# Linear attention on one core: split float32r projections, a longer look-ahead, and rewritten engine lists with the inter-state products in one piece

## The reference, cut to what matters

```python
        def chunk_gla(q, k, v, gk, C=CHUNK):
            g = jnp.cumsum(gc, axis=1)
            g_last = g[:, -1]
            qg = qc * jnp.exp(g)
            kg = kc * jnp.exp(-g)
            A = jnp.einsum('cthd,cshd->chts', qg, kg)
            A = A * jnp.tril(jnp.ones((C, C), q.dtype))
            o_intra = jnp.einsum('chts,cshe->cthe', A, vc)
            k_out = kc * jnp.exp(g_last[:, None] - g)
            chunk_kv = jnp.einsum('cthd,cthe->chde', k_out, vc)
            decay = jnp.exp(g_last)

            def step(S, inp):
                kv, dec, qg_c = inp
                o_inter = jnp.einsum('thd,hde->the', qg_c, S)
                return (S * dec[..., None] + kv, o_inter)
```

## Time and profile before

| what | us |
|---|---|
| median of 3 runs | 5345.69 (5344.24 to 5350.46) |
| span of the profiled execution, first to last instruction | 5273.1 |
| median less this span | 72.6 |
| PE, DVE, ACT, POOL busy in the span | 4750.9, 4145.9, 3061.5, 1117.5 |
| linear attention, from its first DMA at 4320.5 to the end of the span | 952.6 |

### The profile page before, as it was taken

How to read it: one execution, slowest core, us unless ns; L and a number is a source line. 1 busy time by engine, 2 the same in 40 slices (tenths; PEclk the granted TensorE clock), 3 DMA queues, 4 the chain that set the end, 5 groups by cost and what they waited for, 6 DMA issues and landing times. The chain is left out here.

```text
span 5273.1 us, 101047 instructions
## 1 busy us (share of the span) xinstructions
PE 4750.9 (90%) x39176; PEld 2433.6 (46%) x39176; DVE 4145.9 (79%) x5059; ACT 3061.5 (58%) x5260; POOL 1117.5 (21%) x1152
## 2 busy tenths in 40 slices
PE   5579999999999999999999988558999969999998
PEld 3223333333333333333333356435666646666666
DVE  4489999999999999999999233377765447877877
ACT  1138888888888888888888712112222225555554
POOL 0000011202112021121211220254420004344443
PEclk8669999999999999999999999879999979999999
DMA  5434422322222222222221127632210030110100
GB/s 181 132 98 138 138 87 88 97 76 82 85 72 81 74 84 77 70 85 72 85 75 55 36 83 237 206 94 74 61 50 9 3 130 24 30 29 25 30 27 18
DMA packets 236953, 421.64 MB, mean 80 GB/s; under 512 B 36745, under 2 KB 141210, under 8 KB 236432
## 3 DMA queue, kind: packets, MB, share of 16 engines
q1 hardware_dynamic: 189680, 341.85, 21.0%
q0 software_dynamic: 30048, 66.76, 4.1%
q10 hardware_dynamic: 16896, 8.39, 0.7%
HBM read 324.51 MB, written 129.17 MB: 86 GB/s over the span
## 5 line engine op out<-in xcount | busy, mean ns | idle before, releaser
L956 DVE TENSOR_REDUCE attn_mpart<-attn_ps_max 128x2 f32<-128x1024 f32 x2048 | 2474.7, 1223 | 94.8 <-PE attn_ps_max L1007 85.1
L821 ACT ACTIVATE attn_probs<-attn_ps_exp 128x512 f32<-128x512 f32 x4096 | 2230.6, 595 | 411.0 <-PE attn_ps_exp L1023 331.3
L1007 PE MATMUL attn_ps_max<-attn_keys,attn_quer 54*128 54x512 f32 x4096 | 1474.0, 461 | 104.5 <-DVE attn_mpart L956 62.4
L1023 PE MATMUL attn_ps_exp<-attn_quer,attn_keys 54*128 54x512 f32 x4096 | 1513.3, 448 | 21.8 <-DMA attn_quer<-m_rows 20.7
L1038 PE MATMUL attn_ps_out<-attn_probs,attn_vals 128*32 128x256 f32 x16384 | 1312.1, 392 | 9.8 <-ACT route_o L826 9.2
L1023 PEld LDWEIGHTS attn_ps_exp<-attn_quer,attn_keys 54*128 54x128 f32 x4096 | 620.0, 185 | 860.1 <-ACT attn_probs L821 769.3
L1038 PEld LDWEIGHTS attn_ps_out<-attn_probs,attn_vals 128*32 128x32 f32 x16384 | 323.6, 108 | 750.8 <-issue 416.4
L1007 PEld LDWEIGHTS attn_ps_max<-attn_keys,attn_quer 54*128 54x128 f32 x4096 | 589.5, 189 | 169.7 <-DVE attn_mpart L956 106.0
L577 POOL DMA_INDIRECT x_rows<-route_pay,route_now x256 | 252.3, 985 | 431.7 <-DMA x_rows<-route_pay,route_now 359.5
L1576 POOL DMA_INDIRECT ra_rows<-y_rows,slots x256 | 255.5, 998 | 316.2 <-DVE ra_total L1743 244.5
L1707 ACT ACTIVATE ra_row<-ra_psS 128x512 f32<-128x512 f32 x112 | 66.9, 597 | 369.9 <-PE ra_psS L1628 369.9
(11 more groups left out here) (367 smaller groups left out, 5394.2 us busy)
## 6 DMA issues: line engine op xcount, KB each, us to landing
attn_keys<-k_laid SPq DMA_DIRECT2D x256, 304.0 KB
attn_vals<-v_aug SPq DMA_DIRECT2D x128, 512.0 KB, 16.1
attn_keys<-k_laid SPq DMA_DIRECT2D x256, 128.0 KB
x_rows<-attn_zeros POOLq DMA_DIRECT2D x16, 1280.0 KB, 10.4
exp_x<-x_rows SPq DMA_DIRECT2D x64, 320.0 KB
exp_w1w<-in_w SPq DMA_DIRECT2D x64, 256.0 KB
y_rows<-exp_y SPq DMA_DIRECT2D x64, 256.0 KB
q_laid<-proj_parts SPq DMA_DIRECT2D x32, 256.0 KB
```

The costliest lines, as they stand in the source:

```text
L821: act.activation(probs[k % 2][:, j, :], ps_exp[bank_of(g, n)][:, :], ACT.Exp).then_inc(exp_done, 1)
L956: dve.tensor_reduce(mpart[i][:, kb, TC * pair + tile::TC * NPR], ps_max[buffer][:, :, :], AX, ALU.max).then_inc(unit_read, 1)
L1007: mm = pe.matmul(ps_max[buffer][:, h, :], quer[at % NG][half(h), pair, tile * P:(tile + 1) * P], keys[at % 2][half(h), pair, kb * CH:(kb + ...
L1023: pe.matmul(ps_exp[bank_of(g, n)][:, :], keys[g % 2][half(h), pair, k * P:(k + 1) * P], quer[g][half(h), pair, :], start=True, stop=True). ...
```

## The change

Six things are changed together.

1. The projections run in float32r from split operands. Every weight and input is cut into a high part (rounded) and the rest: one float32 matmul of 512 columns becomes two or three float32r ones (Z1, Z2 become one each, on operands stacked along the rows). The weights are split at the end of `low_rank` on ACT and POOL, `low_rank` stores the low-rank columns already split (12 DMAs a chunk instead of 1), and in each iteration ACT and POOL split the input (`hch`, `hcl`), ACT and DVE the log-sigmoid (`lsh`, `lsl`).
2. `inter` runs on 64 rows a head: the states of two heads no longer stand in a wide block with zeros, so DVE scales 1280 columns once instead of twice, and PE runs 40 matmuls of 64 columns on half the rows in place of 20 of 128 columns.
3. The key-value products and decay sums move to the PSUM of the output; the dense state is added apart from those of the experts (`add_dense`, `add_experts`), and intra waits for it.
4. The output's residual is read back from DRAM (`x_mid`, stored by `rope_attention`), the gate of the output is folded into `wo`, and the space of `xres` holds keys and states.
5. The look-ahead is one iteration longer (`far`): Z1, Z2 and ZG of the tile after next stand at the end of the list.
6. The lists have another order. On PE: features, scores, K2, Q2, decay sums, key-value products, V, scores, turned output, intra, G1, G2, output product, K1, Q1, the whole of `inter` in one piece, then Z1, Z2, ZG. On ACT and DVE see below.

```diff
+class GlaWeights:
+
+
+    def __init__(self, keep):
+        self.qkv = [keep("gw_qkv" + n, [P, 3, KD, KDV], F32R) for n in ("_high", "_low")]
+        self.up = keep("gw_up", [P, UPS, KDV], F32R)
+        self.cen = keep("gw_cen", [P, P], F32R)
...
+                for dst, src in ((qkv[:, :, :, :], w_qkv), (up[:, :, :], w_up),
+                                 (gw.wo[:, :, :], w_o.rearrange("(a p) d -> p a d", p=P)),
...
+                        for g, r in ((0, LOW_G1[1]), (1, LOW_G2[1])):
+                            for x, part in enumerate((high, rest, high)):
+                                sp.dma_start(lz_d[g, x * GLR:(x + 1) * GLR, n],
+                                             part[r:r + GLR, 1, :].bitcast(F32)).then_inc(low_stored[i], 16)
+                        for x, (b, r) in enumerate((LOW_GATE, LOW_K, LOW_Q)):
+                            for y, part in enumerate((high, rest)):
+                                sp.dma_start(lg_d[y * LORA:(y + 1) * LORA, x, n],
+                                             part[r:r + LORA, b, :].bitcast(F32)).then_inc(low_stored[i], 16)
...
+                act.wait_ge(g_loaded, 112)
+                act.wait_ge(tri_step, 5)
+                act.activation(gw.qkv[0][:, :, :, :], qkv[:, :, :, :], ACT.Copy).then_inc(w_high, 1)
+                act.activation(gw.up[:, :, :], up[:, :, :], ACT.Copy).then_inc(w_high, 1)
...
+        psS = pb("psS", [P, 2 * CH])
+        kve = psS[:, :].rearrange("p (a e d) -> p a e d", a=NPAIR, e=NE)
+        psO = pb("psO", [P, 2, CH])
+        heads_out = psO[:, :, 0:KDV // 2].rearrange("p o (b d) -> p b o d", b=NPAIR)
+        kvd = psO[:, 0, KDV // 2:KDV].rearrange("p (a d) -> p a d", a=NPAIR)
+        pdec = psO[:, 1, KDV // 2:KDV // 2 + NPAIR * NS * 2].rearrange("p (a e c) -> p a e c", a=NPAIR, e=NS)
...
-                def iteration(nxt, cur, prv):
-                    copy_feats(cur)
+                    act.activation(of_pairs(sq[:, :, :]), heads_out, ACT.Square, scale=DK ** -0.5).then_inc(squared, 1)
+
+                def iteration(far, nxt, cur, prv):
+                    if prv is not None:
+                        square(prv)
+                    if cur is not None:
+                        copy_feats(cur)
                     if nxt is not None:
-                        log_sigmoids(nxt, cur)
-                    else:
+                        copy_gate(nxt)
+                    if cur is not None:
                         decays(cur)
                     if nxt is not None:
+                        log_sigmoids(nxt)
                         q2_and_v(nxt)
+                        split_ls(nxt)
                     if prv is not None:
                         copy_o(prv)
                     if nxt is not None:
                         exps(nxt)
-                    square(cur)
-
-                def prologue(tile):
-                    log_sigmoids(tile, None)
-                    q2_and_v(tile)
-                    exps(tile)
+                    if far is not None:
+                        split_h(far)
...
+                def split_ls(tile):
+                    m, _, i = tile
+                    dve.wait_ge(ls_high, m + 1)
+                    dve.wait_ge(projected, NP * m)
+                    dve.tensor_tensor(lsl[:, :, :], ls[i][:, 0:2, :], lsh[:, :, :].bitcast(F32),
+                                      ALU.subtract).then_inc(ls_low, 1)
...
-                def iteration(nxt, cur, prv):
+                def iteration(far, nxt, cur, prv):
                     if prv is not None:
                         mean_square(prv)
-                    if nxt is not None:
-                        add_bias(nxt)
-                        center(nxt)
-                    mask_scores(cur, 0)
-                    if prv is not None:
+                        age(prv)
                         scale_o(prv)
                         gated(prv)
-                    mask_scores(cur, 1)
+                    if cur is not None:
+                        mask_scores(cur, 0)
+                    if nxt is not None:
+                        center(nxt)
+                    if cur is not None:
+                        decay_states(cur)
                     if nxt is not None:
                         log_sigmoid(nxt)
-                    decay_states(cur)
-                    add_to_states(cur)
+                    if cur is not None:
+                        mask_scores(cur, 1)
+                        add_dense(cur)
+                    if nxt is not None:
+                        split_ls(nxt)
+                    if cur is not None:
+                        add_experts(cur)
+                    if nxt is not None:
+                        normalised_keys(nxt)
                     if prv is not None:
                         output(prv)
                     if nxt is not None:
-                        scaled(nxt)
-
-                def prologue(tile):
-                    add_bias(tile)
-                    center(tile)
-                    log_sigmoid(tile)
-                    scaled(tile)
+                        sparse_feats(nxt)
+                        dense_feats(nxt)
+                        gate(nxt)
+                    if far is not None:
+                        add_bias(far)
...
-                        if item == G1:
-                            pe.wait_ge(ls_ready, m + 1)
                         x = item - G1
-                        mm = pe.matmul(ps, (cen[:, :], m2c[i][:, 1, :])[x], ls[i][:, x, :], start=True, stop=True)
+                        pe.wait_ge(ls_low, m + 1)
+                        for part in (lsh, lsl):
+                            mm = pe.matmul(ps, (cen[:, :], m2g[i][:, :])[x], part[:, x, :], start=(part is lsh),
+                                           stop=(part is lsl))
                     elif item in (Q1, K1, V):
                         x = {Q1: 0, K1: 1, V: 2}[item]
+                        if item == V:
+                            pe.wait_ge(h_low, m + 1)
                         for k in range(KD):
-                            mm = pe.matmul(ps, hc[i][:, k, :], wqkv[:, x, k, :], start=(k == 0), stop=(k == KD - 1))
+                            for h_part, w_part in ((hch, wqkv[0]), (hch, wqkv[1]), (hcl, wqkv[0])):
+                                mm = pe.matmul(ps, h_part[:, k, :], w_part[:, x, k, :], start=(k == 0 and w_part is wqkv[0]
+                                               and h_part is hch), stop=(k == KD - 1 and h_part is hcl))
+                    elif item in (Z1, Z2):
+                        mm = pe.matmul(ps, lcz[i][:, :], wup[:, (UP_Z1, UP_Z2)[item - Z1], :], start=True, stop=True)
                     else:
-                        (b, r), rows = {Z1: (LOW_G1, GLR), Z2: (LOW_G2, GLR), ZG: (LOW_GATE, LORA), K2: (LOW_K, LORA),
-                                        Q2: (LOW_Q, LORA)}[item]
-                        mm = pe.matmul(ps, lc[i][r:r + rows, b, :], wup[r:r + rows, b, :], start=True, stop=True)
+                        x, blocks = {ZG: (0, (UP_GATE, UP_GATE_LOW)), K2: (1, (UP_K, UP_K_LOW)),
+                                     Q2: (2, (UP_Q, UP_Q_LOW))}[item]
+                        for n, block_ in enumerate(blocks):
+                            mm = pe.matmul(ps, lcg[i][:, x, :], wup[:, block_, :], start=(n == 0), stop=(n == 1))
...
+                    pe.wait_ge(dec_exped, m + 1)
+                    for odd in (1, 0):
+                        if odd == 0:
+                            pe.wait_ge(dense_read, m + 1)
...
+                    for b in pairs:
                         for e in range(NS):
-                            queries = qeT[:, b, e - 1, :] if e else ftT[:, 1, b, :]
-                            mm = pe.matmul(o, queries, s_mid[:, b, e, :, :].rearrange("p h d -> p (h d)"),
-                                           start=False, stop=(b == NPAIR - 1 and e == NE), skip_group_check=True)
-                    mm.then_inc(intra_inter, 1)
-
-                def iteration(nxt, cur, prv):
+                            for odd in range(2):
+                                rows = slice(odd * DK, odd * DK + DK)
+                                queries = qeT[rows, b, e - 1, :] if e else ftT[rows, 1, b, :]
+                                mm = pe.matmul(heads_out[:, b, odd, :], queries, s_mid[rows, b, e, :], start=False,
+                                               stop=(b == NPAIR - 1 and e == NE), skip_group_check=True)
...
                     ahead = lambda *items: [project(nxt, x) for x in items] if nxt is not None else None
-                    ahead(Z1, Z2)
-                    turn_feats(cur)
-                    ahead(ZG, K2)
-                    scores(cur, 0)
-                    decay_sums(cur)
-                    scores(cur, 1)
-                    ahead(Q2, V)
+                    if cur is not None:
+                        turn_feats(cur)
+                        scores(cur, 0)
+                    ahead(K2, Q2)
```

(49 more changed lines are left out.)

279 lines of the change are left out of this document (176 added, 103 removed).

## The result

The changed kernel takes 5501.15 us (median of 4 runs, 5483.66 to 5525.49). Beside the kernel before on the same chip (5344.97) the ratio is 1.0293, 95% interval 1.0255 to 1.0331: +156 us. The forecast was 5465 and slower. A second measurement on another chip gave 1.0297 (1.0257 to 1.0337).

What follows compares the result with a forecast made beforehand. PE sets the pace, but the new order of the lists decides the cycle: 31 x (32.2 - 28.40) = +118, fixed terms +6, on 5345.7, less 5 for the last iterations, gives 5465 us; range 5385 to 5525.

Steps and rivals of the forecast that it cites:

- The walk: One linear-attention iteration followed through the new lists with measured durations: cycle 30.2 us against 27.96, PE idling some 3.5.
- The clock: Linear-attention loop: PE's waits lower the granted clock, priced 2.0 us an iteration, between none and 3.25; likeliest cycle 32.2.
- The loop: 31 linear-attention cycles at 32.2 us instead of 28.40: +118 us.
- Float32r and `inter`: PE in linear attention: float32r rows of 512 columns at 0.23 us each; `inter`'s 80 rows in 4.5 us.
- the bound of 9.0: Upper estimate for `inter`: 80 rows at today's 0.112 us a row, 9.0 us.
- the 8.5 of loads one behind the other: `inter`: 80 weight loads of 128 columns without overlap, an estimated 8.5 us, half rows saving nothing.
- PE's sum: PE's busy time in one linear-attention iteration: from 26.9 to about 24.1 us.
- DVE's scaling: DVE in linear attention: two state scalings of 1.50 us become one, saving 1.5 us.
- The fixed terms: `x_mid` store +4, `low_rank` DMAs +2, ACT's weight high halves +6.6, linear attention's start about 6.5 shorter: together +6 us.
- B: Linear-attention order costs 2 us a cycle but the clock falls no further: +56 and +6, 5408 us; chance 0.20.
- C: Shorter ACT and DVE chain in linear attention, PE's smaller sum decides: cycle 26.0, 5278 us; chance 0.13.
- E: `inter`'s weight loads do not overlap within a head pair, or more clock is lost: 5527 us and more; chance 0.06.

Runs made afterwards that it cites:

- the kernel with the products twice: Changed kernel with the key-value products made a second time behind the second scores, same result: 1.0351 of the kernel before.
- the kernel before with late masks: Kernel before with only DVE's log-sigmoid put ahead of the second masks: 1.0136 of the kernel before.
- decays behind exp: Changed kernel with one ACT instruction moved, the decay exponential behind exp instead of ahead of |z|: 1.0038 of the kernel before.
- the kernel with the masks moved: Changed kernel with DVE's second masks put ahead of the log-sigmoid, ACT's early decay exponential kept: 1.0146 of the kernel before.
- The ageing move: Decays behind exp, plus DVE's ageing of the states moved from the next iteration's head to between gate and bias: 1.0006 of the kernel before.
- the last kernel: Changed kernel with decay exponential behind exp, ageing late, `inter` in two pieces, router's exponential ahead of the weights' copies: 5262.27 us, 0.9962 of the kernel before.

## Why the prediction held, and where it was off

- **The walk.** Its clock times from the first feature turn (4714.87 after), forecast and measured: decay sums done +6.6, +6.58; |z| begins +6.8, +6.88; ln done +12.5, +12.68; second masks done +15.6, +15.67; `lsl` done +17.2, +17.14; K1 +20.5, +22.48; `inter` ends +28.1, +30.08. It was exact to 0.2 up to `lsl`. The 2 us come between `lsl` and K1, where intra and the turned output run at the lower clock. There the walk had a wrong link: it hung G1 on `lsl`, but G1 begins at +19.24, 2.1 behind `lsl`, for intra stands ahead of it on PE. At full clock that costs little: in the undisturbed cycles of the kernel with the products twice K1 begins at +20.8, and the cycle is 30.28 where the walk has 30.2.
- **The clock,** +2.0 a cycle, was a choice between 0 and 3.25, and nothing ahead of the run fixed it. Against the 30.28 at full clock the 32.41 measured make it 2.1; that the choice came so near is luck in part. The experiments show that it hangs on PE's waits: 3.48 or 3.71 in one piece lost clock in each round, 2.4 in some (the kernel before with late masks), 1.2 to 1.4 in none (decays behind exp). It isn't a rule by length: with waits under 1 us the kernel with the masks moved still lost some clock in six rounds, and the kernel before in some.
- **The loop:** +120 for 30 cycles against +118 for 31. For the last iterations 5 us were taken off; behind the 31st `inter` the change is 3 us longer instead.
- **Float32r and `inter`.** 0.23 us a row measured (4738.38 to 4738.61), K2 and Q2 1.13 (4719.21 to 4720.34) where the walk has 1.12, `inter` 4.61 against 4.5. Its 80 rows went by at 0.058 each, so neither the bound of 9.0 nor the 8.5 of loads one behind the other came: the loads overlap. PE's sum was a bit low: 24.97 busy at full clock, forecast 24.1.
- **DVE's scaling** was a step that failed, at no cost in the forecast: one instruction instead of two saves not 1.5 us but 0.5, for the one takes 2507 ns (mean of 32) where 1500 stood in the earlier trace rows. It begins at 4722.84, while POOL's products of the queries run until 4724.02; before, POOL was idle beside it. In the chain of waits of the kernel with decays behind exp, it and POOL's slow add both stand in the line that ends in front of PE:

```profile
4747.85 1.28 POOL gla_ms L2330
...
4749.31 1.64 POOL gla_ms L2332
...
4755.17 1.65 DVE xres L2520
```

  The ageing move took 0.28 of the 0.7 by which that cycle lies above the walk. That the scaling holds the rest is likely by these rows, but it was not tried apart.
- **The fixed terms** were mis-sized: +6, measured +21 ahead of the first `inter` and, for the store of `x_mid` (forecast +4), 2 or 7 us of the rotary attention, by the chip. Of the 21, `low_rank`'s chunks are 8.46 us apart (4360.42 to 4368.88, two stores of `hT_d`) where they were 7.10, since ACT waits 5.04 us for the stores of the low-rank columns: +6 in all against +2. The router's piece between the last logits and the first turned mask was priced with the copies alone, +6.6, and took +15.5: 20.57 us (4363.78 to 4384.35) against 5.04 before. Its timeline after:

```profile
4366.30 3.60 ACT L2056 ACTIVATE gw_up<-low_up 128x4096 fp32r<-128x4096 f32 x1
...
4370.28 6.65 POOL L2025 TENSOR_TENSOR gw_qkv_low<-low_qkv,gw_qkv_high 128x3072 fp32r<-128x3072 f32 x1 [3.98 <-ACT gw_cen L2057]
...
4372.47 4.61 DVE L2083 TENSOR_TENSOR low_probs<-low_probs,low_total 128x128 f32<-128x128 f32 x1
4377.11 3.42 POOL L2031 TENSOR_TENSOR gw_up<-low_up,gw_up 128x1536 fp32r<-128x1536 f32 x1 [0.18 <-POOL gw_qkv_low L2025]
...
4377.43 3.24 DVE L2086 TENSOR_TENSOR emask<-low_probs,erw 128x128 f32<-128x128 f32 x1
```

  DVE's products of 128 x 128 end when POOL's splits end, 4.61 and 3.24 us for what takes 0.29 in the last kernel, where POOL starts its splits behind them: there the piece is 6.46 us (4290.40 to 4296.86). The sum priced ACT's part of this splitting and put POOL's at nothing; that was the failed step. The start of linear attention saved the forecast 6.5 (first DMA to first product 4419.65 to 4428.45, 8.8 us where it was 15.3), and from there to the first `inter` 5.7 were given back (52.65 against 46.95).
- **Rivals.** B needed the clock at 1.00 and C a logarithm at +10.5; neither came. A cycle of 28.2, where C begins, is what the kernel with one instruction moved shows. E's loads did not come.

## What to carry to other kernels

In a list written by hand, ask of every instruction that waits for another engine what stands behind it, ready: the cheapest instruction of ACT's list, 0.2 us, cost 136 us by its place. Walk one cycle with measured durations before trusting the sums of busy time: PE had 2 us less to do, and the cycle grew by 4. Two delays that are harmless or cheap apart can meet in one long wait of PE, and the clock then charges for it once more; so move what makes the wait, or split it. Filling it works only as far as nothing else breaks: here the wait went and the full clock came back, but PE stopped for 3 us in another place. When a run misses all expectations, list the engine's idle stretches by length first, those without a releaser too.

## What the runs showed of the hardware

- An elementwise instruction of DVE whose two operands both come from SBUF and one of POOL did not run side by side: POOL's add took 200 ns undisturbed and 1272 beside DVE's ageing, the ageing 1482 where it began first and 2324 beside POOL's masked keys, a product of 128 x 128 in `low_rank` 0.29 us alone and 4.61 beside POOL's split. The Trainium skill, "SBUF — State Buffer", section "Who interferes with whom", says that a DVE instruction with two SBUF inputs contends with a GpSimd instruction that reads SBUF, and that the order of issue decides which of two contending instructions is held up. The traces agree, for both orders. DVE's masks, which read PSUM, kept their 0.68 us beside POOL.
- The granted clock fell to half behind stops of PE of over 3 us, with a releaser or without: 3.48 us for DVE's masks in the changed kernel, 3.22 us without a releaser in the kernel with the products twice, where it stayed at half for 10.24 us. It fell at times with no such stop too: in six of 28 rounds of the kernel with the masks moved, whose waits for DVE are 0.78, 0.85 and 0.96.
- A PE loop made longer by 80 products and their 80 weight loads a tile stopped for 3.1 to 3.6 us, with no releaser in the profile, each of the 13 times that it went round again. The cause is open.
- The same stage with the same instructions took 823 or 866 us by the chip. The mean granted clock was 0.93 and 0.91, and some 15 of the 43 us lie where it was 1.00 on both.
